# First attention with VectorE's share of the weight sums as strided sums over buffers of their own, and a middle stage with 128-row operands

## What is computed

```python
x = x + tanh(g_xattn[0]) * L0_xattn(ctx, layernorm(x), mask, ...)   # first attention
x = x + tanh(g_ffn[0]) * L0_ffn(layernorm(x), ...)                  # experts (middle stage)
x = x + tanh(g_xattn[1]) * L1_xattn(layernorm(x), ctx, ...)         # second attention
x = x + tanh(g_ffn[1]) * L1_ffn(layernorm(x), ...)                  # quantised layer

# L0_xattn: 16 heads of 64; keys and values from both the normed ctx and the normed x
q = ln(x) @ Wq;  k, v = split(concat([ln(ctx), ln(x)]) @ Wkv)
w = softmax(where(mask, q k^T * scale, -max));  out = (w @ v) @ Wout
# L0_ffn: softmax(x @ router_w + router_b), the best two of 8 experts,
#         sum over experts of weight * (gelu(x @ W1 + b1) @ W2 + b2), 128 hidden units each
# L1_xattn: 16 heads of 16; q = x @ Wq.T + bq, k = ctx @ Wk.T + bk, v = ctx @ Wv.T + bv
```

## Time and profile before

| | |
|---|---|
| time, median of 3 runs | 3391.27 us (3391.16 to 3396.19) |
| profiled execution | 3392.96 us |
| its span in the trace | 3391.1 us, mean granted TensorE clock 0.956 |
| TensorE (PE) busy | 3001.4 us, 89% |
| VectorE (DVE) busy | 2453.9 us, 72% |
| GpSimd (POOL) busy | 2082.1 us, 61% |
| ScalarE (ACT) busy | 1817.4 us, 54% |
| first attention | from about 176 to 2394 us in the span |
| middle stage | from 2394 to about 2606 us |

### The profile page before, as it was taken

The page is one execution under the profiler, slowest core; times in us unless marked ns, Lnnn a source line. Parts: engine busy times, 40 slices in busy tenths (PEclk is TensorE's granted clock), DMA queues, the critical chain, the costliest instruction groups (busy, mean ns, idle before and its releaser), DMA issues. The chain is left out here.

```text
span 3391.1 us, 53618 instructions
## 1 busy us (share of the span) xinstructions
PE 3001.4 (89%) x21696; PEld 1101.4 (32%) x21704; DVE 2453.9 (72%) x3029; ACT 1817.4 (54%) x2033; POOL 2082.1 (61%) x968
## 2 busy tenths in 40 slices
PE   3589999999999999999999999998697799999947
PEld 1223333333333333333333333322354133333324
DVE  5567777778767877778777876782535888888758
ACT  3155445555555545544555555544443588888833
POOL 0077898888888889879888888989510111111022
PEclk9699999999999999999999999999698799999969
DMA  1000000000000000000000000000210100000000
GB/s 59 5 1 1 1 7 1 1 1 7 1 1 7 1 1 7 1 1 7 1 1 1 2 1 1 1 1 1 74 23 13 42 7 6 7 8 6 4 0 26
DMA packets 24536, 28.72 MB, mean 8 GB/s; under 512 B 6431, under 2 KB 21216, under 8 KB 24290
## 3 DMA queue, kind: packets, MB, share of 16 engines
q1 hardware_dynamic: 24290, 25.30, 2.6%
HBM read 17.42 MB, written 2.10 MB: 6 GB/s over the span
## 5 line engine op out<-in xcount | busy, mean ns | idle before, releaser
L413 POOL TENSOR_TENSOR a_acc_p<-a_acc_p,a_prob 128x1024 f32<-128x1024 f32 x704 | 1726.1, 2452 | 299.5 <-ACT a_prob L483 217.8
L543 DVE TENSOR_REDUCE a_part_max<-wide 128x2 f32<-128x1024 f32 x896 | 1088.4, 1215 | 475.6 <-PE wide L713 474.9
L483 ACT ACTIVATE a_prob<-slot,a_mask_bias 128x1024 f32<-128x1024 f32 x928 | 987.6, 1113 | 732.1 <-PE slot L738 712.7
L753 PE MATMUL bank<-a_prob,a_val 128*64 128x512 f32 x3712 | 898.8, 606 | 2.1 <-ACT a_prob L483 2.1
L713 PE MATMUL wide<-a_k_hi,a_q_hi 64*128 64x512 f16 (+1 forms) x2048 | 365.9, 369 | 147.4 <-DVE a_part_max L543 134.9
L1025 ACT ACTIVATE a_prob<-slot,a_mask_bias 128x1024 f32<-128x1024 f32 x416 | 455.4, 1116 | 65.5 <-PE slot L1183 52.2
L1067 DVE TENSOR_REDUCE a_part_max<-wide 128x1 f32<-128x512 f32 x514 | 332.7, 681 | 37.3 <-PE wide L1171 20.4
L753 PEld LDWEIGHTS bank<-a_prob,a_val 128*64 128x64 f32 x3712 | 226.6, 136 | 394.9 <-issue 290.2
L738 PE MATMUL slot<-a_q_hi,a_k_lo 64*128 64x512 f16 x1856 | 353.1, 377 | 0.0
L738 PE MATMUL slot<-a_q_hi,a_k_step_hi 64*128 64x512 f16 x1728 | 328.7, 377 | 2.6 <-ACT a_prob L483 2.5
L738 PE MATMUL slot<-a_q_lo,a_k_step_hi 64*128 64x512 f16 x1728 | 328.3, 377 | 0.0
(11 more groups left out here) (367 smaller groups left out, 3284.6 us busy)
## 6 DMA issues: line engine op xcount, KB each, us to landing
a_w_staged<-in_w SPq DMA_DIRECT2D x8, 384.0 KB, 3.2
x_res<-in_x SPq DMA_DIRECT2D x1, 2048.0 KB, 9.1
a_q_op<-a_hi SPq DMA_DIRECT2D x128, 16.0 KB, 1.8
out_x<-x_res SPq DMA_DIRECT2D x16, 128.0 KB
a_k_op<-mid_k_hi SPq DMA_DIRECT2D x32, 52.0 KB, 2.2
mid_context<-in_ctxt SPq DMA_DIRECT2D x1, 1601.0 KB, 6.6
mid_w_staged<-in_w1a SPq DMA_DIRECT2D x4, 385.0 KB, 4.2
ctx_rows<-in_ctx SPq DMA_DIRECT2D x1, 1536.0 KB
```

Source lines behind the costliest of these rows:

```text
L413: nc.gpsimd.tensor_tensor(acc, before, prob[:, k % R, :], ALU.add).then_inc(added_p, 1)
L483: nc.scalar.activation(prob[:, k % R, :], m.slot[k % 2][:, :], ACT.Exp, bias=mbias[:, t:t + 1]).then_inc(probs_ready, 1)
L543: nc.vector.reduce_max(part_max[:, w % 2, :, j, c], pairs, AX.X).then_inc(max_used, 1)
L753: ins = nc.tensor.matmul(av[r, :], val[g % 2][:, t, r], prob[:, k % R, h * QB:(h + 1) * QB], start=(t == 0), stop=(t == NT - 1), tile_posi ...
```

## The change

It has two parts.

In the first attention VectorE no longer sums tile by tile. Six tiles of a unit, in two batches (2, 5, 8) and (15, 18, 21), get buffers of their own, `a_own[:, 1]` to `[:, 3]`, into which ScalarE writes the exponential; they don't pass through the ring. VectorE sums a batch by `fold`: one `reduce_sum` over the tile axis for each quarter of the columns. The first batch is summed into `own[:, 0]` (three inputs for each output, 768 elements a piece) at steps 10 to 13; the second together with `own[:, 0]` into `own[:, 4]` (four inputs, 1024 elements) at steps 23, 24, 25 and 27. Consecutive inputs of one output lie 4096 bytes apart. GpSimd sums 23 tiles, with one accumulator, and `add_up` moves from step 2 to step 1 and writes to `own[:, 4]`, which `sums` reads. The inversions move to steps 14 to 17, the product to 18, the outputs to 19 and 21. The evacuation of the key projections (ScalarE and VectorE) is done in pieces of 256 columns.

In the middle stage the job order becomes keys of group 0, values of all groups, keys of groups 1 to 3. The keys' bias becomes a seventh matmul of each key job, so that ScalarE evacuates a key job once, and `k_low` goes to VectorE, which reads the other half from PSUM. The bias operand, `mid_ones`, `mid_pick`, `mid_wt_hi` and `mid_wt_lo` get 128 rows, zeros where there was nothing; GpSimd writes the zeros. The bias and group 1's weights are loaded ahead of the large expert weights. `c_split` and `w_split` are done in two instructions each (the second for keys and values, `mid_kv_lo`, and queries, `a_wq_lo`), all `ones_of` stand at the end of GpSimd's program, ScalarE takes its evacuations in another order with the experts' high halves later, and `first(0)`, `first(1)` come behind the turned routing weights.

```diff
-        self.sums_at, self.invert_at, self.pieces, self.divide_at, self.out_at = 9, 12, 4, 16, (17, 19)
+        self.sums_at, self.invert_at, self.divide_at, self.out_at = 9, (14, 15, 16, 17), 18, (19, 21)
+        self.pieces = len(self.invert_at)
         self.last_pair, self.turn_at = 24, 25
-        self.dve_tiles = [5, 7, 9, 15, 17]
-        self.pool_tiles = [t for t in range(self.nt) if t not in self.dve_tiles]
+        self.batches, self.fold_at = ((2, 5, 8), (15, 18, 21)), ((10, 11, 12, 13), (23, 24, 25, 27))
+        self.folds = len(self.fold_at[0])
+        self.pool_tiles = [t for t in range(self.nt) if not any(t in b for b in self.batches)]
...
-        acc_v, acc_p = sb("acc_v", [P, 2, 2 * QB]), sb("acc_p", [P, 2, 2 * QB])
...
+        own, acc_p = sb("own", [P, 5, 2 * QB]), sb("acc_p", [P, 2 * QB])
...
+        ring_tiles = [(w, t) for w in range(a.units) for t in a.pool_tiles]
+        ring_place = {what: n for n, what in enumerate(ring_tiles)}
+
+        def weights_of(w, t):
+            if a.batch_of(t) is not None:
+                return own[:, 1 + a.batch_of(t)[1], :]
+            return prob[:, ring_place[w, t] % R, :]
...
-                if n == 0 and w >= 2:
-                    pool.wait_ge(den_ready, w - 1)
+                if n == 0 and w:
+                    pool.wait_ge(total_ready, w)
...
             def add_up(w):
-                pool.wait_ge(added_v, adds_v * (w + 1))
+                pool.wait_ge(folded, folds * (w + 1))
                 pool.wait_ge(added_p, adds_p * (w + 1))
-                acc = acc_p[:, w % 2, :]
-                nc.gpsimd.tensor_tensor(acc, acc, acc_v[:, w % 2, :], ALU.add).then_inc(total_ready, 1)
+                nc.gpsimd.tensor_tensor(own[:, 4, :], acc_p[:, :], own[:, 4, :], ALU.add).then_inc(total_ready, 1)
...
-                    if w and t == 2:
+                    if w and t == 1:
...
-                if k >= R:
-                    act.wait_ge(av_done, k - R + 1)
-                    v, s = divmod(k - R, NT)
-                    if s in a.pool_tiles:
+                mine = a.batch_of(t)
+                if mine is None:
+                    n = ring_place[w, t] - R
+                    if n >= 0:
+                        v, s = ring_tiles[n]
+                        act.wait_ge(av_done, v * NT + s + 1)
                         act.wait_ge(added_p, adds_p * v + max(a.pool_tiles.index(s), 1))
-                    else:
-                        act.wait_ge(added_v, adds_v * v + max(a.dve_tiles.index(s), 1))
-                nc.scalar.activation(prob[:, k % R, :], m.slot[k % 2][:, :], ACT.Exp, bias=mbias[:, t:t + 1]).then_inc(probs_ready, 1)
+                elif w or mine[0]:
+                    v, b = (w, mine[0] - 1) if mine[0] else (w - 1, len(a.batches) - 1)
+                    act.wait_ge(av_done, v * NT + a.batches[b][mine[1]] + 1)
+                    act.wait_ge(folded, folds * v + a.folds * (b + 1))
+                nc.scalar.activation(weights_of(w, t), m.slot[k % 2][:, :], ACT.Exp, bias=mbias[:, t:t + 1]).then_inc(probs_ready, 1)
...
-            def add(w, t):
...
-                nc.vector.tensor_tensor(acc, before, prob[:, k % R, :], ALU.add).then_inc(added_v, 1)
+            def fold(w, b, piece):
+                if piece == 0:
+                    dve.wait_ge(probs_ready, w * NT + a.batches[b][-1] + 1)
+                    if b and w:
+                        dve.wait_ge(den_ready, w)
+                    dve.wait_ge(folded, folds * w + a.folds * b)
+                c = slice(piece * 2 * QB // a.folds, (piece + 1) * 2 * QB // a.folds)
+                src = own[:, 0 if b else 1:4, c].rearrange("p r c -> p c r")
+                nc.vector.reduce_sum(own[:, 4 if b else 0, c], src, AX.X).then_inc(folded, 1)
...
-                    if t - 2 in a.dve_tiles:
-                        add(w, t - 2)
-                    elif w and t + NT - 2 in a.dve_tiles:
-                        add(w - 1, t + NT - 2)
+                    for b, steps in enumerate(a.fold_at):
+                        if t in steps:
+                            fold(w, b, steps.index(t))
...
+        kinds = [("k", 0)] + [("v", g) for g in range(self.groups)] + [("k", g) for g in range(1, self.groups)]
+        self.jobs = [(g, kind, c) for kind, g in kinds for c in range(nc)]
...
+        kv_hi, kv_lo = sb("kv_hi", [P, a.groups, 2 * DC * P], FP16), sb("kv_lo", [P, a.groups, 2 * DC * P], FP16)
+        bias, bias_hi, bias_op = sb("bias", [2, 2, a.groups * P]), sb("bias_hi", [2, 2, a.groups * P], FP16), sb("bias_op", [P, 2, a.groups * P], FP16)
+        ones = sb("ones", [P, 512], FP16)
...
-        pick = sb("pick", [NE, NE, P], FP16)
+        wt_h, wt_l = sb("wt_hi", [P, TOK], FP16), sb("wt_lo", [P, TOK], FP16)
+        pick = sb("pick", [P, NE, P], FP16)
...
+            sp.dma_start(bias[:, :, :].rearrange("p k c -> p (k c)"), bias_in[0:1, :].broadcast_to([2, 2 * a.groups * P])).then_inc(bv_loaded, 16)
+            sp.dma_start(w_st[:, 1, :], w_in[1, :, :]).then_inc(w_loaded[1], 16)
             for dst, source in fetch[a.small:]:
                 sp.dma_start(dst, source).then_inc(fetched, 16)
-            sp.dma_start(bias[:, :], bv_in[0:1, :].broadcast_to([2, a.groups * P])).then_inc(bv_loaded, 16)
-            for g in range(1, a.groups):
-                if g >= 2:
-                    sp.wait_ge(w_lo, g - 1)
+            for g in range(2, a.groups):
+                sp.wait_ge(w_lo, g - 1)
...
-                if k >= a.y_ring:
-                    act.wait_ge(k_split, k - a.y_ring + 1)
                 if g >= 2:
                     act.wait_ge(laid[g % 2], a.laid_group * (g // 2))
-                b = keep.qk_bias[:, g, 1:2]
-                nc.scalar.activation(y[:, k % a.y_ring, 0:w], jbank(p)[:, 0:w], ACT.Identity, bias=b, scale=1.0 / WSCALE).then_inc(y_set, 1)
-                nc.scalar.activation(k_hi[:, g % 2, at:at + w], jbank(p)[:, 0:w], ACT.Identity, bias=b, scale=1.0 / WSCALE).then_inc(evacuated, 1)
+                nc.scalar.activation(k_hi[:, g % 2, at:at + w], jbank(p)[:, 0:w], ACT.Copy, scale=1.0 / WSCALE).then_inc(evacuated, 1)
...
+            def k_low(p):
+                g, _, c = a.jobs[p]
+                at, w = a.chunks[c]
+                dve.wait_ge(evacuated, p + 1)
+                if g >= 2:
+                    dve.wait_ge(laid[g % 2], a.laid_group * (g // 2))
+                nc.vector.scalar_tensor_tensor(k_lo[:, g % 2, at:at + w], jbank(p)[:, 0:w], 1.0 / WSCALE, k_hi[:, g % 2, at:at + w],
+                                               ALU.mult, ALU.subtract).then_inc(k_split, 1)
...
+                own_bias = bias_op[:, 0 if kind == "k" else 1, g * P:(g + 1) * P]
                 if kind == "k":
                     for q, (wt_, x) in enumerate(passes):
                         for d in range(DC):
-                            col = (DC + d) * P
-                            ins = nc.tensor.matmul(out[:, 0:w], wt_[:, g, col:col + P], x[:, d, at:at + w],
-                                                   start=(q == 0 and d == 0), stop=(q == 2 and d == DC - 1))
+                            nc.tensor.matmul(out[:, 0:w], wt_[:, g, d * P:(d + 1) * P], x[:, d, at:at + w], start=(q == 0 and d == 0), stop=False)
+                    ins = nc.tensor.matmul(out[:, 0:w], own_bias, ones[:, 0:w], start=False, stop=True)
                 else:
-                    pe.wait_ge(bias_ready, 1)
                     for b in range(w // P):
                         own = out[:, b * P:(b + 1) * P]
-                        nc.tensor.matmul(own, ones[:, :], bias_op[:, g * P:(g + 1) * P], start=True, stop=False)
                         for q, (wt_, x) in enumerate(passes):
                             for d in range(DC):
-                                col = (2 * DC + d) * P
-                                ins = nc.tensor.matmul(own, x[:, d, at + b * P:at + (b + 1) * P], wt_[:, g, col:col + P],
-                                                       start=False, stop=(q == 2 and d == DC - 1))
+                                nc.tensor.matmul(own, x[:, d, at + b * P:at + (b + 1) * P], wt_[:, g, (DC + d) * P:(DC + d + 1) * P],
+                                                 start=(q == 0 and d == 0), stop=False)
+                        ins = nc.tensor.matmul(own, ones[:, 0:P], own_bias, start=False, stop=True)
...
+            for p in range(NC, NC + a.routing):
                 project(p)
-            first(0)
-            first(1)
-            project(12)
-            project(13)
             pe.wait_ge(weights_done, 1)
             for g in range(NB):
                 if g >= 2:
                 for j in range(4):
                     ins = nc.tensor.transpose(sbank(g)[0:NE, j * P:(j + 1) * P], wt[:, 4 * g + j, :], m.ident[:, :])
                 ins.then_inc(wt_turned, 1)
-                project(14 + g)
-            for p in range(14 + NB, a.nj):
+                project(NC + a.routing + g)
+            first(0)
+            first(1)
```

(27 more changed lines are left out.)

173 lines of the change are left out of this document (84 added, 89 removed).

## The result

The changed kernel takes 3425.58 us (median of 4 runs, 3422.09 to 3429.40) where the kernel before takes 3391.22: a ratio of 1.0098, 95% interval 1.0081 to 1.0116. The forecast was 3359, faster. The profiled execution took 3423.97 us, its span is 3422.1. The page's second part after hardly differs from the earlier trace rows: slices of 86 us are too coarse to show where the time went.

The account below looks back on a forecast made before the run. TensorE bounds the first attention, held back 101.7 us by VectorE's reductions that empty `wide`. Terms -15 - 4 - 3 - 4 - 6 = -32 us from the profiled execution gave 3359 us; range 3332 to 3455, the forecast's own 3335 to 3382.

Parts of the forecast that it names:

- The price of a piece: First attention, VectorE: strided reads cost nothing extra, so three-input pieces take 0.95 us and four-input pieces 1.22.
- R1: Rival, first attention: every strided element costs 0.8 ns more, pieces of 1.57 and 2.04 us; 3490 us, chance 0.19.
- A rule against this change: First attention: documented penalties for hopping reads would make pieces 1.5 and 1.9 us, the kernel about 3445 us.
- The first batch, forecast free: First attention, steps 10 to 13: pieces of 0.95 us beside each reduction cost TensorE nothing.
- The four places of the second batch: First attention: pieces cost about 0.5 us at step 24, 1.1 at 25, and are hidden at 23 and 27.
- GpSimd's end: Last unit of the first attention: one sum less and less lateness on GpSimd shorten TensorE's final wait, -4 us.
- The middle stage, -13: Middle stage: three pieces, the start -3, the projections -4 and the experts -6 us.
- The value blocks: Middle-stage projections: bias matmuls with 128 rows take their neighbours' time, 52 x 0.19 = -9.9 us.
- the spread: Middle-stage experts: spread matmuls with 128 rows save 0.19 us in each of 32 steps, -6 us.
- The start: Middle stage's start: earlier bias load and halved weight splits, between 0 and -6, taken as -3 us.
- the forecast's upper case: Middle-stage projections: with the wait for key copies on the path, the projections' term can be +5 instead of -4 us.
- R2: Rival, first attention: 0.4 ns more an element, 3.8 us added a unit; 3420 us, chance 0.11.

Follow-up runs that it names:

- e0: Kernel before plus a leading stage of VectorE reductions alone, 2 to 6 inputs: three apart take 0.94 us, four apart 1.79.
- e3: Changed kernel with the second batch's pieces reading three inputs, not four, leaving the first batch's sum out of the denominators: 3370.59 us (0.9933).
- e8: e4 with the first batch moved to tiles 2, 4, 7 and its pieces to steps 9, 11, 12, 13: 3322.59 us (0.9789).
- e4: Changed kernel with second batch of tiles 15, 18 plus the first's sum, pieces at steps 20 to 23, tile 21 on GpSimd: 3345.72 us (0.9866).
- e6: Kernel before with an unused four-input piece added behind shift_of at step 25 in 31 units: 3457.26 us (1.0194).
- e5: Changed kernel with the second batch's third piece at step 26 instead of 25: 3395.52 us (1.0009).
- e9: Changed kernel with the first batch alone on VectorE, the other 26 tiles on GpSimd: 3373.31 us (0.9928).
- e2: Kernel before's first attention with the changed middle stage: 3379.50 us (0.9962).
- e7: Kernel before's first attention and the changed middle stage, its bias and spread operands read with few rows again: 3402.60 us (1.0037).

## Why the prediction was wrong, point by point

- **What bounds the stage** was right: TensorE's waits for the reduction of `wide` carried the result.
- **The price of a piece is the step that failed.** One rate was taken for all pieces, and both ends of the bound (0 and 0.8 ns an element) were held to go for both batches. The truth was one end for each: three inputs 1.03 us, four 1.96 (e0, e3). R1's price of 2.04 us was nearly right for the second batch, and wrong for the first (1.57). It was not the whole error: with three-input pieces of 1.03 us at the same steps (e3) the stage ends 9.3 us earlier than before, where the sum had 19 us with pieces of up to 1.22. Moving the first batch (e8) gave back 23 us, more than the difference.
- **"A rule against this change"** quoted the Trainium skill's "Advanced Engine Details and Errata", section Memory Cachelines, by which each access to another line pays, and the Trainium skill's "Vector Engine (DVE) Microarchitecture Reference", section 5.2, for the price of a source that hops at every element. From the latter the estimate was 1.9 us for the second batch, which took 1.96, and 1.5 for the first, which took 1.03. In e0 each element pays from four inputs on, 0.65 ns; with two none does (0.60 us apart and adjacent), with three hardly (0.94 against 0.86). The case that the same section of the Trainium skill reports, two regions at the full rate, agrees with the 0.60 us, and was the hint that the number of regions counts.
- **The first batch, forecast free:** a piece is 0.08 us longer than a reciprocal, so the reductions come every 2.08 us (pieces start at 1053.16, 1055.23 and 1057.31), not 1.95: 0.13 us a step. In units with `a_k_lo` at step 10 the collision cost far more (seven waits of 2.0 us in the changed kernel and in e4, none in e8; the `a_k_lo` of 2.27 us shown in the last section stands ahead of one), and the prediction had not seen it; e8 removed it, for 23 us.
- **The four places of the second batch:** 0.5, 1.1 and nothing at steps 23 and 27. The reading that a piece behind `shift_of` costs its whole length was right, with 1.96 in place of 1.22: e6 measures 1.7 us of waits for it, e5 the 30 us that moving it gives back. The cover at 23 and 27 wasn't tested by itself.
- **The clock was left out of the attention,** a term put at nothing without a reason. TensorE fell to half clock eleven times, each time behind a wait of 1.9 us or more; 15.5 us of the loss by the windows. The waits came first: e3, which shortens the long pieces, has three of the falls left.
- **GpSimd's end, -4:** 1.0 us. By the kernel's waits the ring of six, not the number of tiles, sets how far GpSimd can be behind; the wait at the end is 15.4 us with 24 tiles (e4) and with 26 (e9).
- **The middle stage, -13:** -13 in the runs (e2), -14.5 and -14.6 in the traces of e2 and of the changed kernel. The value blocks (-9.9: 8.1 in e7) and the spread (-6: -7.5 in e7, -7.8 in the trace of e2) were sized well. The start, -3, was a loss instead: the first key job comes 16.3 us behind the first transposition in the changed kernel and 14.3 before, since the bias operand is now waited for. The wait for the key copies came, as the forecast's upper case had it: ScalarE's evacuation of the last group stands 6.27 us for the copies, and TensorE 4.40 us for what follows from it.
- **R2**, 3420 us, came within 6 us of the time by luck: its middle price, 0.4 ns an element, is that of neither batch. Its terms add up to 3.9 us a unit and not 3.8. It was given 0.11.

## What to carry to other kernels

When a strided read has no row in the trace, measure it by itself for each count of streams before building an order on it: here three inputs were nearly free and four cost 1.9 times as much. A unit of work on an engine off the critical path should be placed by what the step has left, and what can't be hidden should go into many short waits rather than into a long one: each fall of TensorE's clock in the first attention that was looked at here stood behind a wait of 1.9 us or more, and e8, whose longest wait for the reductions is 1.3 us, has none. Giving the second batch three inputs in place of four and moving the pieces of both batches was worth 103 us: 55 came with the third input (e3, whose sums are incomplete), 25 with the second batch's places and 23 with the first's.

## What the runs showed of the hardware

VectorE's sum of 1024 columns with two sources in SBUF takes 1.22 us alone (e0) and 2.27 in the kernel before, where GpSimd sums beside it. `a_k_lo`, a subtraction of the same kind, shows how: in the changed kernel one of 512 columns at 1181.36 takes 0.68 us while GpSimd idles, one of 128 columns at 1196.40 takes 2.27 while GpSimd sums.

```profile
1181.36 0.68 DVE L558 TENSOR_TENSOR a_k_lo<-a_k_step,a_k_step_hi 128x512 f16<-128x512 f32 x1
...
1196.40 2.27 DVE L558 TENSOR_TENSOR a_k_lo<-a_k_step,a_k_step_hi 128x128 f16<-128x128 f32 x1
```

```profile
1196.16 4.85 POOL L431 TENSOR_TENSOR a_acc_p<-a_acc_p,a_prob 128x1024 f32<-128x1024 f32 x2 [1.26 <-ACT a_prob L505]
```

The Trainium skill's "SBUF — State Buffer", section "SBUF: two separate sides", has the rule: a VectorE operation with two inputs in SBUF and a GpSimd operation take a shared pair of ports in turn, each for its whole instruction. The rows agree, and the sums with one source kept their length beside GpSimd: three inputs 1.03 us in e0 and in the kernel, four 1.88 and 1.96. Why the mean of `a_k_lo` with 512 columns rose from 0.95 to 1.50 us with the change was not tried and stays open.
